# Expert rounds: first product moved to place 0, VectorE's loops turned inside a layer, two copies in place of three in the plain steps

## What is computed

```python
x = x + _L0_conv_ref(_ln_c(x), ...)       # attention by softmax over positions
t = t + _L0_ffn_ref(_ln_t(t), ...)        # 8 experts, the best 2 of each token count
x = x + _L1_conv_ref(_ln_c(x), ...)       # grouped 3 x 3 convolution
t = t + _L1_ffn_ref(_ln_t(t), ...)        # an ODE over the positions, below

def _mlp(y, W1, b1, W2, b2, W3, b3):
    h = jnp.tanh(y @ W1.T + b1)
    h = jnp.tanh(h @ W2.T + b2)
    return h @ W3.T + b3
def _rk4_step(y, dt, params):
    k1 = f(y)
    k2 = f(y + dt / 2 * k1)
    k3 = f(y + dt / 2 * k2)
    k4 = f(y + dt * k3)
    return y + dt * (k1 + 2 * k2 + 2 * k3 + k4) / 6
y0 = x[:, 0]
_, ys = jax.lax.scan(interval, y0, None, length=S - 1)
```

## Time and profile before

| | |
|---|---|
| median of 3 runs | 2909.33 us (2907.96 to 2913.87) |
| the profiled execution's own time | 2912.94 us |
| its span, from the first to the last instruction | 2911.1 us |
| busy share of PE, DVE, ACT, POOL | 97%, 83%, 52%, 20% |
| chain that ended last, share by engine | PE 92%, DVE 4%, ACT 2%, issue 2% |
| mean granted clock of TensorE | 0.98 of full speed |

### The profile page before, as it was taken

One profiled execution on the slowest core, in us unless ns is written; L12 is line 12 of the kernel. 1 busy time (PEld: TensorE's weight loads), 2 busy tenths in 40 slices (PEclk: granted clock), 3 DMA queues, 4 the chain that ended last, 5 costly groups with the idle time before them and its releaser, 6 DMA issues.

```text
span 2911.1 us, 204519 instructions
## 1 busy us (share of the span) xinstructions
PE 2822.3 (97%) x80498; PEld 2406.9 (83%) x80498; DVE 2408.5 (83%) x13418; ACT 1521.8 (52%) x10124; POOL 585.3 (20%) x903
## 2 busy tenths in 40 slices
PE   7789999999999999999999999999999999999999
PEld 3468888888888888888888887888889999999998
DVE  4668888888888888888888887888888888888888
ACT  5445555555555565555554444444445555555554
POOL 5023323333233233233232000111110000000000
PEclk8779999999999999999999999999999999999999
DMA  3000000000000000000000000000000000000000
GB/s 117 0 8 16 11 11 14 11 12 13 11 14 11 11 14 11 11 14 11 11 14 8 1 0 1 0 0 0 0 17 0 0 0 0 0 0 0 0 0 14
DMA packets 21982, 28.21 MB, mean 10 GB/s; under 512 B 4384, under 2 KB 12896, under 8 KB 21544
## 3 DMA queue, kind: packets, MB, share of 16 engines
q1 hardware_dynamic: 21928, 27.48, 3.1%
HBM read 25.24 MB, written 2.23 MB: 9 GB/s over the span
## 4 chain that ended last, share of the span: by engine, by line
PE 92%; DVE 4%; ACT 2%; issue 2%; DMA 0%; SPq 0%; DVEq 0%; ACTq 0%; POOLq 0%; POOL 0%
PE PSUM L646 22%; PE PSUM L652 20%; PE PSUM L833 14%; PE PSUM L707 12%; PE PSUM L829 6%; PE PSUM L637 5%; PE PSUM L814 3%; PE PSUM L808 2%; DVE PSUM L1334 1%; PE PSUM L744 1%; PE PSUM L673 1%; ACT HA L1017 1%; PE PSUM L677 1%; PE PSUM L714 1%; PE PSUM L484 1%
## 5 line engine op out<-in xcount | busy, mean ns | idle before, releaser
L1334 DVE TENSOR_REDUCE PSUM<-PSUM 128x32 f32<-128x64 f32 x2912 | 624.4, 232 | 98.4 <-PE PSUM L652 52.3
L646 PEld LDWEIGHTS PSUM<-HA,RL 128*128 128x128 f16 x11648 | 396.6, 96 | 205.8 <-ACT HA L1017 194.9
L1018 ACT ACTIVATE PSUM<-PSUM 128x32 f32<-128x32 f32 x2912 | 562.2, 194 | 0.0
L1017 ACT ACTIVATE HA<-PSUM 128x32 f16<-128x32 f32 x1456 | 287.8, 198 | 469.0 <-DVE PSUM L1334 468.9
L1017 ACT ACTIVATE HB<-PSUM 128x32 f16<-128x32 f32 x1456 | 288.0, 199 | 467.4 <-DVE PSUM L1334 467.4
L646 PE MATMUL PSUM<-HA,RL 128*128 128x16 f16 x11648 | 512.1, 170 | 15.4 <-ACT HA L1017 7.6
L646 PE MATMUL PSUM<-HB,RLU 128*128 128x16 f16 x11648 | 511.4, 170 | 4.6 <-ACT HB L1017 0.2
L652 PE MATMUL PSUM<-HA,RH 128*128 128x32 f16 x11648 | 465.2, 177 | 0.0
L652 PE MATMUL PSUM<-HB,RHU 128*128 128x32 f16 x11648 | 464.4, 177 | 0.0
L415 POOL TENSOR_TENSOR G<-G 128x512 f16<-128x512 f32 x256 | 296.3, 1157 | 684.1 <-ACT G L990 684.1
L646 PEld LDWEIGHTS PSUM<-HB,RLU 128*128 128x128 f16 x11648 | 394.0, 96 | 47.9 <-ACT HB L1017 2.4
(11 more groups left out here) (293 smaller groups left out, 6932.0 us busy)
## 6 DMA issues: line engine op xcount, KB each, us to landing
G<-scores SPq DMA_DIRECT2D x64, 256.0 KB, 3.1
N<-in_x SPq DMA_DIRECT2D x8, 256.0 KB, 5.8
NHL<-in_w SPq DMA_DIRECT2D x1, 2048.0 KB, 10.4
STF<-in_w SPq DMA_DIRECT2D x1, 2048.0 KB, 15.1
out<-W2HL SPq DMA_DIRECT2D x8, 256.0 KB, 2.4
G<-in_r SPq DMA_DIRECT2D x1, 1024.0 KB, 5.3
R1K<-in_r SPq DMA_DIRECT2D x1, 256.0 KB, 2.7
R3F<-in_r SPq DMA_DIRECT2D x1, 256.0 KB, 5.5
```

The costliest lines, as they stand in the source:

```text
L646: mm(out[m // 2][:, 2 * B * (m % 2):2 * B * (m % 2) + B], lo[:, k, m], src[:, k, 0], start=False, stop=False)
L1017: A(hi[:, 2 * h:2 * h + 2, 0], src, ACT.Tanh, scale=1.0 / scale).then_inc(rk_hi, 1)
L1018: A(full, src, ACT.Tanh, scale=1.0 / scale).then_inc(rk_f, 1)
L1334: v.tensor_reduce(bank[:, SUM:SUM + 2 * B].rearrange("p (m b) -> p m b", m=2), bank[:, 0:4 * B].rearrange("p (m c b) -> p m b c", m=2, c=2 ...
```

## The change

Three constants are changed, one product is taken out, and DVE's round is cut at another point.

- `PER_SLOT` gives slot 0 one product and slot 8 one in place of two. So each of the first twelve products of a round stands one position earlier, and the product without a reader in slot 0 (L686) is gone. A round on PE has 24 products of 512 columns in place of 25.
- `EDGE` is 10, and `step` has two ranges, `sums` and `rest`, in place of one. A round's opening part ends after the sums and the subtractions of place 10; the update of VS of that place, and what stands beside it, come after the turn.
- `COPIES` is 2: products of 32 columns in place of 48, injects of 128 and 64 in place of 192 and 96.

```diff
-PER_SLOT = (0, 2, 2, 1, 2, 1, 2, 1, 2, 2, 2, 1, 2, 1, 2, 1)
+PER_SLOT = (1, 2, 2, 1, 2, 1, 2, 1, 1, 2, 2, 1, 2, 1, 2, 1)
-EDGE = 11
+EDGE = 10
-COPIES = 3
+COPIES = 2
...
                 if slot == 0:
-                    mm(PS[6][:, :], CKH[:, 0:128], CKL[:, 0:TILE], start=True, stop=True)
                     at[0] = (g % NE) * MC if isinstance(g, int) else pe.snap((g % NE) * MC)
                     at[1] = g // NE if isinstance(g, int) else pe.snap(g // NE)
...
-            def step(s, first, beside=lambda slot: None, r=0, layers=range(8)):
+            def step(s, first, beside=lambda slot: None, r=0, sums=range(8), rest=range(8)):
                 for j in range(4):
                     for lay, hi in ((0, HA), (1, HB)):
-                        if 2 * j + lay not in layers:
-                            continue
-                        for h in range(2):
+                        for h in range(2) if 2 * j + lay in sums else ():
...
-                        for h in range(2):
+                        for h in range(2) if 2 * j + lay in sums else ():
...
+                        if 2 * j + lay not in rest:
+                            continue
...
-            def part(s, beside, begin, end):
+            def places(begin, end, r):
+                return range(max(begin - 8 * r, 0), min(end - 8 * r, 8))
+
+            def opening_part(s, beside):
                 for r in range(2):
-                    inside_step = range(max(begin - 8 * r, 0), min(end - 8 * r, 8))
-                    if len(inside_step):
-                        step(s + r, False, beside, r, inside_step)
+                    step(s + r, False, beside, r, places(0, EDGE + 1, r), places(0, EDGE, r))
+
+            def closing_part(s, beside):
+                step(s + 1, False, beside, 1, places(EDGE + 1, SLOTS, 1), places(EDGE, SLOTS, 1))
```

More of the change, by code:

```diff
@@ L1336, in step @@
                                             AX.X, ALU.add).then_inc(rk_r, 1)
-                        if lay == 0 and j == 0 and not first:
+                        if lay == 0 and j == 0 and not first and 0 in sums:
                             dve.wait_ge(rk_s, 4 * s)
                             summed_low()
-                        for h in range(2):
+                        for h in range(2) if 2 * j + lay in sums else ():
                             dve.wait_ge(rk_f, count(s, j, lay, h))
@@ L1380, in _ @@
             step(0, True)
-            def part(s, beside, begin, end):
+            def places(begin, end, r):
+                return range(max(begin - 8 * r, 0), min(end - 8 * r, 8))
+            def opening_part(s, beside):
                 for r in range(2):
-                    inside_step = range(max(begin - 8 * r, 0), min(end - 8 * r, 8))
-                    if len(inside_step):
-                        step(s + r, False, beside, r, inside_step)
+                    step(s + r, False, beside, r, places(0, EDGE + 1, r), places(0, EDGE, r))
+            def closing_part(s, beside):
+                step(s + 1, False, beside, 1, places(EDGE + 1, SLOTS, 1), places(EDGE, SLOTS, 1))
             def rounds(start, count, beside):
-                part(start, beside(0, True), 0, EDGE)
+                opening_part(start, beside(0, True))
                 with dve.Fori(0, count - 1) as i:
-                    part(start + 2 * i, beside(i, False), EDGE, SLOTS)
-                    part(start + 2 * (i + 1), beside(i + 1, False), 0, EDGE)
-                part(start + 2 * (count - 1), beside(count - 1, False), EDGE, SLOTS)
+                    closing_part(start + 2 * i, beside(i, False))
+                    opening_part(start + 2 * (i + 1), beside(i + 1, False))
+                closing_part(start + 2 * (count - 1), beside(count - 1, False))
             def experts_beside(g, opening):
```

## The result

| | before | after |
|---|---|---|
| median (6 runs each) | 2909.11 us (2907.96 to 2913.87) | 2925.49 us (2924.11 to 2926.66) |
| the profiled execution's own time | 2912.94 us | 2926.66 us |
| ratio after to before | | 1.0053, 95% interval 1.0043 to 1.0063 |

A forecast was written before the change was run, and what follows sets the result against it. The prediction took the chain of sums (DVE), tanh (ACT) and products (PE) as the bound, plus PE's overhang in some slots; +10.4 + 2.1 - 4.1 = +8.4 us gave 2917.7 us, with 2903 to 2925 for 8 in 10.

The forecast's parts named there:

- Sign and place: Whole kernel: slower by 8.4 us, the expert stage a little slower and the plain stage a little faster; chance 60%.
- Slots 0 and 1: Expert rounds: address computations make slot 0 0.28 us late, slot 1 gives some back; 63 x 0.165 = +10.4 us.
- rival 1: Slot 0: PE's address computations hide, its product starting before 301.70; 2901.6 us, faster; chance 17%.
- The step that failed: Expert slots: products standing one position earlier cost 0, each wait for a gelu being met already.
- DVE's turn: Turn of DVE's loop, 85 times: the VS update now stands behind it, 0.025 us each, +2.1 us.
- Rival 2: DVE's turn hides in its wait for ACT, -8.5 us there; 2907.1 us, no change; chance 12%.
- Two copies: 73 plain steps: narrower injects save 0.056 us a step, -4.1 us.
- Rival 4: Plain steps give more or less and slot 1 gives more back; some 2913 us, no change; chance 8%.
- The product without a reader and the one taken out of slot 8: Slots 0 and 8: both products fill PE's waits, so removing them saves 0.
- rival 3: Plain steps: granted clock falls to the 1.2 GHz level, 7% of 735 us, +51 us, 2969; chance 3%.

The follow-up runs named there:

- fixed_address: order_kept with slot 0's product reading weights and activations at a fixed address, its computations back in slot 1; 2904.84 us, ratio 0.9978 to the kernel before.
- product_only: Kernel before with the product moved to slot 0, the change's table and no product without a reader; 2928.51 us, ratio 1.0067.
- order_kept: product_only with one product each in slots 0 and 1, all others where they stood before; 2920.3 us, ratio 1.0034 to the kernel before.
- turn_only: Kernel before with DVE's turn inside layer 10 (EDGE = 10) alone; 2912.17 us, ratio 1.0008.
- filler_only: Kernel before without the product that has no reader, its table kept; 2911.95 us, ratio 1.0002.
- later_by_one: Kernel before with slot 1's second product moved to slot 7, the product without a reader kept; 2906.59 us, ratio 0.9982.
- combined: Kernel before with COPIES = 2 and the second products of slots 1 and 14 moved to slots 7 and 15; 2899.79 us, ratio 0.9965.
- combined_hinted: combined with three rounds of DVE's expert loop per turn and a prefetch hint; 2899.97 us, ratio 0.9954 to the kernel before.
- three_rounds: Kernel before with three rounds per turn in DVE's expert and convolution loops; 3024.61 us, ratio 1.0392.

## Why the prediction was right in its direction and short in its size

- **Sign and place.** Right: the expert rounds got slower, the plain steps faster. The measured median, 2925.49, is 0.5 us above the range's upper end, 2925. Against the profiled execution of before, +13.7 measured stands for +8.4 forecast. That the median fell so near the range is luck: the range rests on three terms, and what is missing is in none of them. Nor is its upper end worked out: the bounds that the prediction gives for its three terms add to +28.6 us, not to the +15 of 2924.
- **Slots 0 and 1: right.** 0.30 late in slot 0 (forecast 0.28); 0.178 a round for both (forecast 0.165), 11.2 us. fixed_address shows that the computations are the whole of slot 0's 0.26, and with them falls rival 1: the product starts 0.35 behind the injects, so nothing in slot 0 hides them. In slot 1 they do hide, if one product follows in place of two.
- **The step that failed** is the one that gave the other products nothing: "0, as with the products that stand one position earlier", since "each wait for a gelu is met by its time already". The gelu is over when the products come, but only just: it ends at the injects' time, and a product that waits for it starts 0.16 to 0.18 later. As the second of a pair that time lay under the first product; as the first it stands ahead of both, and such a slot had only 0.02 to spare (slot 6 before: 309.51 + 0.43 = 309.94, the layer at 309.96). 0.112 x 63 = 7.1 us, shown by product_only against order_kept. In the stages' sum (+13.8) this alone is more than the whole miss of 5.4; by the ratio's +15.4 the miss is 7.0, and this is all of it. Term by term: 8.4 + 7.1 + 0.8 (slots 0 and 1) - 0.9 (turn) - 0.8 (copies) = 14.6.
- **DVE's turn: right.** 1.473 in place of 1.443 (forecast 0.02 to 0.03 more). What was not seen is that the next interval is 0.011 shorter, so a turn costs +0.019 and not +0.025. turn_only gave +2.3 (-0.3 to +4.9). Rival 2 fell. The 22 turns in the statistics and convolution changed nothing that these stages' sum shows (173.8 + 350.1 before, 173.6 + 350.2 after), so the term is +1.2 in place of +2.1.
- **Two copies: right.** -4.9 us in the stage (forecast -4.1): the layers at 1.281 came to 1.260 and a step's first from 1.306 to 1.267, as forecast. Some 0.5 of the 4.9 is the scatter of single traces: turn_only, product_only, order_kept, fixed_address, filler_only and later_by_one, with three copies, lie at 734.5 to 734.8 us there, and the four with two copies at 730.0 to 730.7.
- **Rival 4** fell too: slot 1 gave back 0.083 a round and the plain steps 4.9 us, both near the forecast.
- **The product without a reader and the one taken out of slot 8: right**, 0 each (filler_only; slots 8 and 9 unchanged).
- **The clock, rival 3,** did not come with two copies, but one step further it does. So the 3% were not wasted on an impossible case. Its size was wrong, some 22 us in place of 51: the 7% of the earlier trace rows are an average over layers of narrow products, 3% longer, and two layers with the statistics' wide ones.

## What to carry to other kernels

When work is dealt over slots, moving an item by one position changes which item stands first behind a wait; list the waits with their new neighbours, and give each wait that is "met already" the time from the release to the issue, here 0.16 to 0.18 us with an address computation behind the wait, before calling it free. Address arithmetic with a division cost nothing where PE's sequencer ran ahead of its array (slot 1 of fixed_address), and 0.26 us a round behind a loop's branch. If a slot overhangs, try pushing its work later into a slot with room before pulling it earlier: slot 1's 0.094 us a round came that way for 0.011 in slot 7.

## What was not expected of the hardware

- A VectorE loop of 157 instructions idles 0.33 us at its turn; one of 465 idles 2.93 and 1.86 us. A branch hint brings that to 0.34 in the expert loop, to 0.70 in a turn of the convolution's, and 2.2 us are paid once where the expert loop ends. TensorE's loop over the same rounds, of some 1270 instructions in the trace (670 without the products), turns with 0.17 us of idle time of its weight loads; why the two engines differ, and what two rounds per turn would give, was not tried.
- With the same products, but 16 columns in place of 32 in 22 of 36 per layer and injects of half the width, the clock fell to its lower level and stayed there, with PE busy over 99% of the time; a layer there is only 3 to 4% longer.
- The layer with the turn of the convolution's loop took 1.430 us in combined and 1.515 in combined_hinted, with nothing changed in the body of that loop, only in the code ahead of it and in how the loop is opened.
- A stall of DVE costs more than itself: in three_rounds TensorE, idle for 2.62 and 1.45 us in the turn shown, went on at a granted clock of 0.50, and the three layers behind took 0.9 us more, on average over the turns.
